# An attention layer on one core: the stretch ahead of the loops rebuilt, and the last heads set in place by TensorE

## What is computed

```python
x = L0_attn_x                                   # (16, 512, 256)
xn = _layernorm(x, axis=-1)
qkv = xn @ w_qkv.T + b_qkv                      # 3 x 16 heads x 16
att = jnp.einsum('bhqd,bhkd->bhqk', q, k) / jnp.sqrt(jnp.float32(hd))
att = att + bias.transpose(2, 0, 1)[None]       # position bias per head
att = jnp.where(causal[None, None], att, -jnp.inf)
att = jax.nn.softmax(att, axis=-1)
out = jnp.einsum('bhqk,bhkd->bhqd', att, v)     # heads joined again
attn = out @ w_proj.T + b_proj
x_q = (xn / s_in).astype(jnp.float8_e4m3fn)     # and the same for the kernel
ffn = (x_q @ k_q) * (s_in * s_k) + ffn_bias     # 256 -> 256
result = x + attn + ffn
```

## Time and profile before

| | us |
|---|---|
| Median of the three runs | 789.04 |
| Their lowest and highest | 788.89, 791.9 |
| The profiled execution, its own time | 790.76 |
| Its span, first to last instruction | 789.0 |
| PE busy in the span | 743.6 (94%) |
| DVE busy | 633.0 (80%) |
| ACT busy | 580.0 (74%) |
| POOL busy | 531.3 (67%) |

### The profile page before, as it was taken

How to read it: one execution, slowest core, us unless ns; L and a number is a source line. 1 busy time by engine, 2 the same in 40 slices (tenths; PEclk the granted TensorE clock), 3 DMA queues, 4 the chain that set the end, 5 groups by cost and what they waited for, 6 DMA issues and landing times.

```text
span 789.0 us, 23171 instructions
## 1 busy us (share of the span) xinstructions
PE 743.6 (94%) x6313; PEld 503.1 (64%) x6313; DVE 633.0 (80%) x2395; ACT 580.0 (74%) x1258; POOL 531.3 (67%) x525
## 2 busy tenths in 40 slices
PE   6879999999999999999999999999999999999983
PEld 3556666676666766666676667666676666666552
DVE  3778788887988888898888888798888889888702
ACT  3337877878787877878787787778787787876760
POOL 6434579677677767677676867767687767767670
PEclk8859999999999999999999999999999999999996
DMA  5603243433443353344524343444335334433202
GB/s 176 240 1 132 101 159 117 157 118 146 169 149 124 122 181 137 112 153 153 171 101 171 115 150 122 148 169 149 124 117 183 134 117 154 155 142 111 88 19 87
DMA packets 55612, 106.07 MB, mean 134 GB/s; under 512 B 10528, under 2 KB 30496, under 8 KB 55584
## 3 DMA queue, kind: packets, MB, share of 16 engines
q1 hardware_dynamic: 54420, 105.05, 37.4%
q10 hardware_dynamic: 1164, 0.68, 0.4%
HBM read 18.68 MB, written 8.91 MB: 35 GB/s over the span
## 4 chain that ended last, share of the span: by engine, by line
PE 74%; DVE 9%; ACT 7%; issue 5%; DMA 2%; DVEq 1%; SPq 1%; POOL 1%; ACTq 0%; POOLq 0%
PE misc_a L669 14%; PE misc_a L553 13%; PE misc_b L553 10%; PE scoreT_b L643 9%; PE scoreT_a L643 5%; PE score_c L620 4%; PE score_a L620 3%; PE misc_b L669 3%; PE misc_b L604 3%; PE scoreT_b L646 2%; ACT qk_parts L837 2%; DVE row_max L1011 2%; PE scoreT_a L646 1%; ACT probs L933 1%; DVE qk_parts L999 1%
## 5 line engine op out<-in xcount | busy, mean ns | idle before, releaser
L1209 POOL TENSOR_SCALAR_AFFINE_SELECT probs<-probs 128x512 f32<-128x512 f32 x256 | 160.0, 636 | 207.8 <-ACT probs L933 204.2
L1011 DVE CUSTOM_DVE_ANT_0 score_b<-score_b,causal_mask_q 128x384 f32<-128x384 f32 (+3 forms) x321 | 163.2, 526 | 89.4 <-PE score_b L620 89.3
L1011 DVE CUSTOM_DVE_ANT_0 score_a<-score_a,causal_mask_q 128x512 f32<-128x512 f32 x319 | 175.7, 568 | 6.5 <-PE score_a L620 3.2
L1011 DVE CUSTOM_DVE_ANT_0 score_c<-score_c,causal_mask_q 128x256 f32<-128x256 f32 (+3 forms) x384 | 172.9, 478 | 3.0 <-PE score_c L620 2.8
L933 ACT ACTIVATE probs<-scoreT_b 128x384 f32<-128x384 f32 (+1 forms) x256 | 132.4, 517 | 43.9 <-PE scoreT_b L646 20.1
L933 ACT ACTIVATE probs<-scoreT_a 128x512 f32<-128x512 f32 (+1 forms) x256 | 143.2, 559 | 6.2 <-PE scoreT_a L646 5.1
L1011 DVE DVE_READ_ACCUMULATOR2_ANT row_max<- 128x1 f32 x1024 | 146.6, 143 | 0.0
L933 ACT ACTIVATE probs<-scoreT_c 128x384 f32<-128x384 f32 (+1 forms) x256 | 133.7, 522 | 3.2 <-PE scoreT_c L646 2.7
L669 PE MATMUL misc_a<-probs,v_ones 128*32 128x128 f32 (+3 forms) x1536 | 128.6, 438 | 2.8 <-DVE xnT_lo L993 1.2
L643 PE MATMUL scoreT_b<-stacks 64*128 64x384 f32 (+3 forms) x320 | 121.2, 398 | 1.8 <-ACT probs L933 1.7
L620 PE MATMUL score_b<-stacks 64*128 64x384 f32 (+3 forms) x321 | 118.5, 401 | 0.3 <-DVE row_max L1011 0.2
(11 more groups left out here) (241 smaller groups left out, 1948.2 us busy)
## 6 DMA issues: line engine op xcount, KB each, us to landing
stacks<-qk_parts SPq DMA_DIRECT2D x128, 512.0 KB, 3.7
x_ring<-in_L_attn_x SPq DMA_DIRECT2D x16, 512.0 KB, 3.5
attn<-out_T SPq DMA_DIRECT2D x63, 128.0 KB, 2.6
xn<-recips SPq DMA_DIRECT2D x31, 256.0 KB
out<-x_ring SPq DMA_DIRECT2D x15, 512.0 KB, 3.0
stacks<-neg_max_T SPq DMA_DIRECT2D x128, 4.0 KB
low_features<-neg_max_T SPq DMA_DIRECT2D x124, 4.0 KB
low_features<-probs SPq DMA_DIRECT2D x8, 128.0 KB, 4.8
```

Of the source, the lines that this page charges most:

```text
L1011: last = V.tensor_tensor_reduce(bank, bank, CMQ[:, T - w:T], 1.0, LEAST, ALU.add, ALU.max, MX[:, g % 2, 8 * h + 4 + qt:8 * h + 5 + qt])
L1209: last = GP.affine_select(out=d, in_=d, compare_op=ALU.is_ge, fill=0.0, base=0, pattern=[[0, HU], [1, P]], channel_multiplier=-1)
```

## The change

Ahead of the loops:

- PE runs seven filling matmuls behind the weights' transposes, and transposes each of the four tiles of the first image as soon as ACT has written it. The split of the transposed image no longer has the bf16 copy ahead of it.
- The first image's four QK evacuations write one copy and then, as an instruction of its own, the second; `QK_lo` waits for the first alone, SP for both.
- The statistics and the normalising of image 1, its T and its evacuations, the first image's quantising, and all 12 chunks of unit 1 stand ahead of the loops. V and the bias's projection move in between the first 12 chunks; filling matmuls stand between the others. The quantising of the FFN weights moves behind the first 12 maxima. Its work tiles and the exponents of image 0 get other memory.
- The first maxima are sent by two DMAs on SP and two on ACT, where ACT sent all four.
- Unit 0 of image 0 has one chunk of each kind in a step, as the other units.

In image 15, PE waits ahead of unit 2 until all maxima are done, and then issues one filling matmul behind each chunk of `scores_T` in units 2 and 3.

At the end there is no regrouping DMA for the last four heads. PE multiplies `out_T` by the odd and by the even columns of the identity, which puts denominators and outputs into rows 64 to 127 of two banks. DVE inverts 64 x 512 denominators and multiplies. Projection, high and low parts go in three pieces (features 0 to 127, 128 to 191, 192 to 255), and the last image's output is stored in four DMAs, two on SP and two on ACT.

```diff
-MT_AT, FIRST_MT_AT = [(0, 3), (1, 3), (2, 3), (3, 3)], (0, 5)
+MT_AT, FIRST_MT_AT = [(0, 3), (1, 3), (2, 3), (3, 3)], (0, 2)
...
-EARLY = 4
-FIRST_UNIT = [[(1 + n // CHUNKS, n % CHUNKS) for n in range(EARLY + a, EARLY + e)]
-              for a, e in [(2 * k, 2 * k + 2) for k in range(8)] + [(16 + k, 17 + k) for k in range(4)]]
...
+            warm(7, STB[2])
+            banks = [misc("T", ct, -2) for ct in range(CT)]
+            for t in range(TT):
+                pe.wait_ge(xn_ready, t + 1)
+                for ct in range(CT):
+                    last = nc.tensor.transpose(banks[ct][:, P * t:P * t + P], XN[:, t, P * ct:P * ct + P], IDF[:, :])
+                    if t == TT - 1:
+                        last.then_inc(t_ready, 1)
...
             for n, c in enumerate(FIRST_CHUNKS):
                 if n == CHUNKS // 2:
                     pe.wait_ge(stack_loaded[0], 32)
                 in_turn(scores(0, 0, c, n))
+                if n in (2, 4):
+                    job_V(0, n // 2 - 1)
+                elif n == 7:
+                    project_bias()
+                else:
+                    warm(1, STB[2])
             pe.wait_ge(ident_steps, 8)
             job_MT(0, 0)
-            for c in range(EARLY):
+            for c in range(CHUNKS):
                 in_turn(scores(0, 1, c))
+                if c == 2:
+                    for ct in range(CT):
+                        job_T(1, ct)
+                else:
+                    warm(1, STB[2])
...
-                        if first and g == 0:
-                            in_turn(scores_T(b, g, k, first), itertools.chain(*(scores(b, i, c) for i, c in FIRST_UNIT[k])))
-                        elif ahead:
+                        if ahead:
                             in_turn(scores_T(b, g, k, first), scores(nb, ng, k))
                         else:
+                            if (g, k) == (2, 0):
+                                pe.wait_ge(max_done, ROW * B)
                             in_turn(scores_T(b, g, k, first))
+                            warm(1, SB_[0])
...
+            pe.wait_ge(ot_ready, 4 * B)
+            for bank, a in ((SB_[2], 1), (STB[2], 0)):
+                mm(bank[64:P, :], IDF[:, a:P:2], OT[:, :], start=True, stop=True).then_inc(ls_ready, 1)
...
+            for n, (rows, ct) in enumerate(((slice(0, P), 0), (slice(0, 64), 1), (slice(64, P), 1))):
+                pe.wait_ge(ah_ready, 2 * B - 1 + n)
+                if n == 2:
+                    pe.wait_ge(lp_done, TT)
+                last_PJ(rows, ct, AH, PH, start=(n == 0))
+                last_PJ(rows, ct, AH, PL)
+                pe.wait_ge(al_ready, B + 1 + n)
+                last_PJ(rows, ct, AL, PH, stop=(n == 2), signal=(None, lp_done, pj_ready)[n])
...
+                act.wait_ge(qk_ready, m + 1)
+                bias = [0, 2, 1, 3][m]
+                A(qk_part(m, 0)[:, 0, :], misc_of("QK", m)[:, :], ACT.Identity, bias=BQ[:, bias:bias + 1]).then_inc(qh_ready, 1)
+                act.wait_ge(qh_ready, m + 1)
+                A(qk_part(m, 0)[:, 1, :], qk_part(m, 0)[:, 0, :].bitcast(F32), ACT.Copy).then_inc(qc_ready, 1)
...
-            send_max(act, 0)
-            act.wait_ge(setup_step, 3)
-            for t in range(TT):
-                normalise(1, t)
+            send_max(act, 0, (2, 3))
+            act.wait_ge(qz_done, 1)
+            for ct in range(CT):
+                XH_evac(1, ct)
+                XB_evac(1, ct)
+            act.wait_ge(kq_made, 1)
...
             dve.wait_ge(small_loaded, 16 * 7)
             then(V.reciprocal(SC[:, 4:5], SC[:, 1:2]))
             then(V.reciprocal(SC[:, 2:3], SC[:, 0:1]))
             then(V.tensor_tensor(SC[:, 3:4], SC[:, 0:1], SC[:, 1:2], ALU.mult))
+            for ct in range(CT):
+                T_lo(0, ct)
+            for t in range(TT):
+                stats(1, t)
+            aggregate(1)
+            QK_lo(0, 0)
...
+            V.tensor_tensor(at[:, 0, :], at[:, 0, :], RB[:, 0, :], ALU.mult).then_inc(div_done, 1)
+            V.tensor_tensor(at[first_half, 1, :], at[first_half, 1, :], RB[first_half, 1, :], ALU.mult).then_inc(div_done, 1)
+            last_lo(0, slice(0, P), 0)
+            dve.wait_ge(ls_ready, 1)
+            V.reciprocal(RB[last_half, 1, :], SB_[2][last_half, :]).then_inc(li_ready, 1)
+            last_lo(1, first_half, 1)
+            dve.wait_ge(ls_ready, 2)
+            dve.wait_ge(li_ready, 1)
+            V.tensor_tensor(at[last_half, 1, :], STB[2][last_half, :], RB[last_half, 1, :], ALU.mult).then_inc(div_done, 1)
+            last_lo(2, last_half, 1)
```

210 lines of the change are left out of this document (97 added, 113 removed).

## The result

The change makes the kernel slower. The median of 20 runs is **801.5 us** (789.54 to 807.47), that of the kernel before beside it 791.72 (20 runs, 788.89 to 794.77). The ratio is 1.0069, 95% interval 1.0045 to 1.0092; it counts only runs within 1.5% of their kernel's fastest, ten of the 20 here, and so is nearer to one than the ratio of the medians, 1.012. The forecast was 776.0, with 782.0 as the end of the range. The time of a run goes with its mean granted clock: 789.54 at 0.993, 795.79 at 0.982, 803.49 at 0.972. Even the quickest run does not beat the quickest of the kernel before (788.89).

The account below looks back on a forecast made before the run. Clock full but for the opening and last slice, so only the opening and last image can change: 11.5 - 0.4 + 2.0 = 13.1 us gained, span 789.0 to 775.9, median forecast 776.0, range 772.5 to 782.

Parts of the forecast that it names:

- First QK and the first pair: Opening: first QK starts at 15.45 us, 2.05 gained; first pair's low part ends at 19.75, 2.8 gained.
- The clock of the first QK: Opening: first QK may run at half clock, 1.4 us for each of two jobs; half of one, 0.7, charged.
- First maximum: Opening: DVE, not the DMA, sets the first maximum, at 25.0 us instead of 29.47; 4.45 gained.
- step 4: Opening: first twelve maxima take 8.7 us with V, bias and nine fillers on PE, ending at 33.7; 3.0 gained.
- fillers' price: Opening and last image: each filling matmul costs 0.22 us; nine in the first maxima cost 2.1.
- step 5: Opening: DVE works from 35.2 to 43.75 us; PE, three chunks ahead, enters the loops at 41.7.
- slower than before: Rival: half clock from first chunk to unit 1, which starts at 71.8 us; total 795, chance 0.03.
- Unit 0 takes 10.3 us: Opening, step 6: PE's products, QK jobs and transposed maxima sum to 10.3 us; unit 1 starts at 52.0.
- The last image loses 0.4: Image 15: wait holds PE 1.56 us, `out_T` comes 0.4 later; ACT paces, hiding the rest of 24 fillers.
- The fillers keep the clock: Image 15: fillers hold the full clock, so the projection takes 1.4 us and not 2.5.
- The tail gains 2.0: Tail: last multiplication ends 1.6 us earlier, with a 3.4 us inversion, plus 0.4 for PE's clock.
- the spread was to land: Tail: spread of the other 12 heads, store right behind, ends between 772.0 and 773.6 us; 773.3 taken.

Follow-up runs that it names:

- after: The kernel with the whole change, against the kernel before; median 801.5 us.
- e1: Changed kernel without the last image's wait and its 24 fillers in units 2 and 3; 795.36 us.
- e2: e1 also without the 20 fillers between the chunks of maxima ahead of the loops; 787.29 us.
- e6: e2 with DVE inverting the last heads' denominators before it waits for the spread inverses; 783.19 us.
- e11: e10 with 14 filling matmuls in the tail, behind the two products that set the heads in place; 782.07 us.
- e12: e11 with the 20 fillers ahead of the loops put back, two behind every second chunk; 782.3 us.
- e8: Changed kernel with all 44 fillers, two behind every second chunk instead of one behind each; 788.59 us.
- e5: e2 with only the wait ahead of unit 2 of the last image put back; 786.22 us.
- e3: Changed kernel with each of the 44 fillers on 64 rows, in the array half the chunk ahead leaves free; 790.33 us.
- e10: e2 with DVE's inversion first and SP's store of image 14's result issued only after the spread inverses landed; 786.88 us.
- e4: Changed kernel with the 44 fillers as full-array products of fp32r weights instead of bf16; 814.01 us.

## Why the prediction was wrong, point by point

1. **First QK and the first pair** (15.45 and 19.75): 15.95 and 20.53. Right within 0.8. The clock of the first QK, charged with a half of 1.4 us, was full through the QK jobs in six of the 13 profiled executions with the new opening (after, e1, e2, e6, e11, e12) and fell ahead of them or within them in the other seven. The term was a fair one. The gap of PE ahead of QK does not decide it alone: full behind 1.86 us (after), 2.13 (e2) and 2.66 (e1), fallen with 2.13 (e8), 2.72 (e5) and 3.8 (e3). What sorts all 13 is the state earlier: the seven fillers behind the weights' transposes took 2.3 to 3.0 us where the clock was full at QK, and 1.67, at the full clock, where it then fell. No run separates the cause. Of the Trainium skill's rule on transposes ("TensorE: Matmul & The Clock Gate", Part 4) no run here is a test either, since eleven fillers stand around the transposes.
2. **First maximum** 25.0: 25.89.
3. **Twelve maxima in 8.7 us** (step 4): they took 11.2. Without the nine fillers they took 9.0 (e2), where the forecast would have had DVE's 7.15: V and the bias's projection hold the chunks up more than the sum of columns had it. The fillers' part, at the full clock, is 2.2 us, 0.25 each. But the **fillers' price** is the step that failed, there a little and in points 4 and 6 by far. It was taken as 0.22 us each, from their columns at the full rate, and those columns were added to the chunks' own. This sum leaves out that the chunks were not one behind the other: of two neighbours, one in each half of the array, both start together. A full-array filler between them makes each run alone, and neither weight load is hidden (in after's rows 0.43 us from chunk to filler and 0.32 from filler to chunk, 0.22 of each the columns).
4. **The loops start at 41.7, DVE paces the 12 chunks ahead of them** (step 5): 53.09. The same price again, at the half clock: 1.16 us for a chunk and filler against DVE's 0.6. From the twelfth maximum to the loops it took 16.0 us, and 9.3 in e2. All in all, from the first maximum to unit 1, 20 fillers cost 37.43 - 29.71 = 7.7 us against e2, 0.39 each, clock included (0.32 at e10's clock). The rival "slower than before" had this mechanism, PE's chunk and filler longer than DVE's step, but it took 0.4 for the two at the full clock and 0.83 at a half, and so put the point of decision at the half clock. The true pair is 0.69 to 0.75 at the full clock and is past DVE's 0.6 already, so its chance of 0.03 was far too low. Its numbers did not come either: unit 1 was to be at 71.8 and came at 63.32, and in the last image, which lost 11.2, it had no more than the forecast's 0.4.
5. **Unit 0 takes 10.3 us**: 10.2. Right by luck: 10.3 was for the full clock, 2.8 us of the 10.2 were at a half, and at the full clock throughout it took 9.6 (e8, e12). Without fillers unit 1 starts at 55.8 (e2), still 3.8 later than the 52.0 of the full clock: 1.1 lies ahead of the first maximum, 1.6 between it and the loops, 1.1 in unit 0, whose first 4.8 us were at a half. So the opening rebuilt, without fillers, gains 8.4 us of the 12.2.
6. **The last image loses 0.4**: it lost 11.2, 1.33 of wait ahead of the mark and 9.8 behind it. "The rest of the 24 fillers hides behind ACT" was the second place of the same mistake; in e5 ACT started exponentials of 512 columns 0.5 us apart, in after it waited for chunks 0.75 apart. "The fillers keep the clock" was wrong too: with them, 10 us of that stretch were at a half, and 6.8 in e5. The wait, thought to cost 1.4, cost 0.5 in the end (e5).
7. **The tail gains 2.0**: 2.04, the right number for a wrong reason (the prediction's list of signs says 16.5 us, its sum 16.0; measured 15.97). The inversion took 3.36 us, forecast 3.4. (By the repeat count that the Trainium skill gives for reciprocal in "VectorE: DVE Perf Modes", section "First, the fixed hardware budget", taken as eight VectorE cycles for each column, an estimate would be 4.3; the measurement stands against it.) But the spread was to land at most 2.6 us after `out_T`. In after that came out, 2.51, only because the fillers had made `out_T` late: it ended 3.9 us behind the issue. Where it ends 2.3 behind, as in the kernel before, the spread lands 4.15 behind it (e2). That is 1.6 of the 2.0 gained; the other 0.4 are the clock, full in after until 5.3 us before the end. The term mis-sized is the spread beside the store, 6.5 us from issue to landing: the 4.27 of the earlier trace rows was one DMA of 128 KB, and this spread is two, of 256 and 128 KB.

The Trainium skill has a rule that would have helped with points 3 and 6. In "TensorE: Matmul & The Clock Gate", Part 3, it says that a weight load overlaps with products in flight only where the row groups differ, and that tiles in different groups run at once. This case agrees in part: chunks in opposite halves start 0.01 us apart (e5), a filler over all rows waits with its load for the chunk (e4), a filler in the other half starts with it (e3). But where all products are over all rows, a load is hidden in spite of the same rows: in e2 the products of V (256 columns, from 24.54) follow each other 0.12 us apart, each with a load of 0.19, and e11's 13 fillers 0.23 apart. What leaves the loads in the open here is the turn between products of 64 and of 128 rows.

What stays open: whether that turn costs because the rows overlap or because the height of the product (64 or 128 rows) changes. The half-height fillers of e3 avoid both, and no run changes one alone. Open too is why the clock fell in the last image in spite of the fillers, while it held at 1.00 in the opening with the pairs (e8, e12) and in the tail (e11). No run separates this from how PE is filled, and each of these is one execution.

## What to carry to other kernels

The price of an added matmul is not its columns but what it does to its neighbours: before you put one between two products, look whether they start together in the trace and whether it has their height (64 or 128 rows of the array); if they do start together, put it behind the pair or into the free half of the array. A filler belongs where an engine truly waits, and its clock gain has to be set against what it delays at either clock. When a term of a sum rests on a transfer, look at what is issued behind it in the new order, not only in the old one.
